# A fused two-layer network on one core: a transposed Q product, K and V in one product, earlier norm statistics, and a packed half tile

## What is computed

```python
x = x + attn(layernorm(x))     # 16 heads of 128, 4 K/V groups, causal softmax, projection
x = x + ternary(layernorm(x))  # a second layernorm, then a product with weights in {-1,0,1}
# linear attention, on layernorm(x):
QKV = einsum('bsd,ed->bse', X, W_in) + b_in
Q, K, V = split(QKV, 3)
Q, K = rope(Q, 128), rope(K, 128)          # only the first 128 of 256 features turn, in pairs
A = sum(K / norm(K) * V, axis=-2)          # one row of 256 numbers per batch
Y = einsum('bsd,ed->bse', A * Q, W_out) + b_out
x = x + Y + X
# gated layer, on layernorm(x), hidden size 704 = 5 tiles of 128 and one of 64:
x = x + qlinear(silu(qlinear(x, gate)) * qlinear(x, up), down)   # integer weights less 128, scaled
```

## Time and profile before

| | |
|---|---|
| median of three executions | 624.9 us |
| profiled execution, its span | 623.68 us, 621.9 us |
| TensorE busy | 582.7 us (94%), 4224 matmuls |
| VectorE busy | 507.0 us (82%), 1546 instructions |
| ScalarE busy | 361.3 us (58%), 1001 |
| GpSimd busy | 230.3 us (37%), 291 |
| share of the chain that ended last | TensorE 70%, VectorE 17%, ScalarE 5%, GpSimd 3% |

### The profile page before, as it was taken

The page is one execution under the profiler, slowest core; times in us unless marked ns, Lnnn a source line. Parts: engine busy times, 40 slices in busy tenths (PEclk is TensorE's granted clock), DMA queues, the critical chain, the costliest instruction groups (busy, mean ns, idle before and its releaser), DMA issues.

```text
span 621.9 us, 13094 instructions
## 1 busy us (share of the span) xinstructions
PE 582.7 (94%) x4224; PEld 545.5 (88%) x4224; DVE 507.0 (82%) x1546; ACT 361.3 (58%) x1001; POOL 230.3 (37%) x291
## 2 busy tenths in 40 slices
PE   8899999999999999999999999989758888799996
PEld 7799999999999999999999999989657777688785
DVE  4789789679878977987897798789969989878764
ACT  5776656656655765665676566568546243454452
POOL 4474223225222321422332142223657777402210
PEclk9999999999999999999999999999978999999998
DMA  8703100000000000000000000000000000001001
GB/s 326 250 1 140 69 2 2 1 1 0 0 0 0 0 0 0 0 0 0 0 0 0 0 0 0 0 2 0 2 1 0 1 1 1 3 1 35 34 14 54
DMA packets 7855, 14.63 MB, mean 24 GB/s; under 512 B 848, under 2 KB 5648, under 8 KB 7696
## 3 DMA queue, kind: packets, MB, share of 16 engines
q1 hardware_dynamic: 7824, 14.23, 6.3%
HBM read 12.13 MB, written 2.10 MB: 23 GB/s over the span
## 4 chain that ended last, share of the span: by engine, by line
PE 70%; DVE 17%; ACT 5%; issue 4%; POOL 3%; DVEq 1%; DMA 0%; ACTq 0%; POOLq 0%
PE bank L518 58%; PE bank L581 4%; PE bank L595 3%; ACT prob L931 3%; PE bank L528 2%; PE bank L598 2%; DVE pT L1165 2%; DVE xn L1159 2%; DVE prob L1384 2%; DVE prob L1231 1%; DVE prob L1210 1%; PE bank L687 1%; DVE stats L1148 1%; DVE ternary_stats L1328 1%; ACT qT L894 1%
## 5 line engine op out<-in xcount | busy, mean ns | idle before, releaser
L420 POOL TENSOR_SCALAR prob<-prob,rowinv 128x128 f32<-128x128 f32 (+1 forms) x128 | 106.5, 841 | 287.2 <-DVE rowinv L1228 287.2
L518 PE MATMUL bank<-xT,big 128*128 128x256 f32 x960 | 125.8, 283 | 0.6 <-DVE xT L1165 0.6
L931 ACT ACTIVATE prob<-prob,negmax 128x128 f32<-128x128 f32 (+1 forms) x256 | 112.9, 444 | 22.3 <-DVE negmax L1222 22.3
L518 PEld LDWEIGHTS bank<-xT,big 128*128 128x128 f32 x960 | 120.2, 192 | 1.5 <-issue 0.8
L518 PE MATMUL bank<-wp,oT 128*128 128x256 f32 x768 | 102.4, 283 | 0.0
L518 PEld LDWEIGHTS bank<-wp,oT 128*128 128x128 f32 x768 | 96.8, 191 | 0.6
L518 PE MATMUL bank<-pT,v 128*128 128x512 f32 (+1 forms) x384 | 81.3, 347 | 16.0 <-DVE pT L1165 13.0
L518 PEld LDWEIGHTS bank<-pT,v 128*128 128x128 f32 x384 | 63.9, 191 | 27.3 <-issue 7.5
L894 ACT ACTIVATE qT<-bank 128x512 fp32r<-128x512 f32 x68 | 40.6, 597 | 74.0 <-PE bank L518 72.5
L1165 DVE TENSOR_TENSOR pT<-bank,pT 128x512 fp32r<-128x512 f32 (+1 forms) x128 | 64.9, 548 | 1.9 <-ACT pT L894 1.9
L1165 DVE TENSOR_TENSOR qT<-bank,qT 128x512 fp32r<-128x512 f32 x68 | 46.8, 688 | 17.5 <-ACT qT L894 17.0
(11 more groups left out here) (132 smaller groups left out, 1038.5 us busy)
## 6 DMA issues: line engine op xcount, KB each, us to landing
x<-in_x SPq DMA_DIRECT2D x8, 256.0 KB, 8.2
raw<-in_wq SPq DMA_DIRECT2D x4, 512.0 KB, 8.2
raw<-in_wp SPq DMA_DIRECT2D x4, 512.0 KB, 8.0
out<-x SPq DMA_DIRECT2D x8, 256.0 KB, 2.1
raw<-in_w_gu SPq DMA_DIRECT2D x1, 1408.0 KB, 8.3
raw<-in_w_in SPq DMA_DIRECT2D x1, 768.0 KB, 4.6
raw<-in_w_down SPq DMA_DIRECT2D x1, 640.0 KB, 7.8
raw<-in_wk SPq DMA_DIRECT2D x1, 512.0 KB, 3.6
```

What stands on the lines that cost most here:

```text
L420: m = pool.tensor_scalar(prob[:, j % 2, 0, a:b], prob[:, j % 2, 0, a:b], rowinv[:, j % 2, r:r + 1], None, ALU.mult)
L518: m = pe.matmul(out, lhs(a), rhs(b), start=first and i == 0, stop=last and i == len(passes) - 1, skip_group_check=True)
L931: m = act.activation(prob[:, j % 2, i, a:b], prob[:, j % 2, i, a:b], ACT.Exp, scale=SCALE, bias=negmax[:, 2 * i + r:2 * i + r + 1], accum_ ...
```

## The change

- The input weights of Q and K are kept with the even features of each rope pair ahead of the odd ones (`by_pairs`, `by_halves`), and so are the rows of W_out. V is in the same order.
- Q is made transposed (features on the partitions) by `linear_q`: 12 matmuls of 256 columns into `bQ`, weights on the stationary side. So y is born transposed, and the transposes of y are gone. The rope of Q works on partitions: `q_products` on VectorE (one instruction of 128x256, two of 64x256), the sum on GpSimd (`q_rotate`). The bias of Q is added per partition.
- K and V are made by one product of 512 columns for each half, with one bias product of 512 columns; the banks alternate between (`bS0`, `bS1`) and (`bT0`, `bT1`) from batch to batch. ScalarE copies K out and squares it straight from PSUM; V stays in PSUM and kv reads it there. kv of batch `n` is made in the call of batch `n`.
- A, the sum of kv, is made as two columns with features on the partitions (`linear_sum`: 4 products of 1 column), copied by ScalarE, and used there as the scale with which Q is turned into the high part of y. The output of batch `n-1` is made in the call of batch `n`.
- The norm statistics of the linear stage are taken in attention: `linear_moments(n-1)` on VectorE and `linear_scale(n-1)` (seven small instructions) on GpSimd in step 7 of batch `n`. The scale and the mean of each batch are kept.
- The low parts of the gate and up weights are made on GpSimd in eight pieces of 352 columns instead of two of 1408; the low parts of the input weights move from VectorE to GpSimd.
- Gate and up of the last hidden tile (64 rows each) are one product of 128 rows. The high and the low part of its hidden values lie above each other in one tile of 128 rows, so one pass of the down product takes both.
- The linear stage is written out instead of a loop; constants for the transposed rope are made in batch 0.

The core of the diff (TensorE, then GpSimd, ScalarE, VectorE):

```diff
+                for k in range(KT):
+                    mm3(pe, out[:, :], lambda a: xTs[n % 2][:, a, k, t * P:(t + 1) * P], lambda a: lin_w[:, a, k, D:3 * D],
+                        k == 0, False)
+                pe.matmul(out[:, :], mean_rows, kv_bias, start=False, stop=True, skip_group_check=True).then_inc(s_kvp, 1)
...
-                for out, a0, a1 in ((bQK[t][:, :], 0, 2 * D), (v_bank(n, t), 2 * D, 3 * D)):
+                    pe.wait_ge(s_lqe, n)
+                    pe.wait_ge(s_lqc, n)
+                for e in range(2):
                     for k in range(KT):
-                        m = mm3(pe, out, lambda a: xTs[q][:, a, k, t * P:(t + 1) * P], lambda a: lin_w[:, a, k, a0:a1],
-                                k == 0, k == KT - 1 and a0 == 0)
-                for a in range(2):
-                    m = pe.matmul(v_bank(n, t), mean_rows, v_bias[:, a, :], start=False, stop=a == 1, skip_group_check=True)
-                m.then_inc(s_lp, 1)
+                        m = mm3(pe, bQ[:, e * S:(e + 1) * S], lambda a: lin_w[:, a, k, e * P:(e + 1) * P],
+                                lambda a: xTs[n % 2][:, a, k, :], k == 0, k == KT - 1)
+                m.then_inc(s_qTp, 1)
...
-                    pe.wait_ge(s_lY, n)
-                for t in range(ST):
-                    m = pe.matmul(bQ[:, 0:D], ones[:, :], kv[:, t, :], start=t == 0, stop=t == ST - 1)
+                if n == 0:
...
+                for e in range(2):
+                    for t in range(ST):
+                        m = pe.matmul(bO[:, e:e + 1], kv[:, t, e * P:(e + 1) * P], ones[:, 0:1], start=t == 0, stop=t == ST - 1)
                 m.then_inc(s_lA, 1)
...
+            def linear(n):
+                if n > 1:
+                    linear_kv(n, 0)
+                linear_transpose(n + 1) if n + 1 < NB else gated_transpose(0)
+                linear_sum(n - 1)
+                linear_kv(n, 1)
+                if n == 2:
+                    pe.wait_ge(s_lAc, n)
                     ternary_transpose(NB - 1)
...
+                if n == 3:
+                    pe.wait_ge(s_lAc, n)
+                    ternary(NB - 1, bO)
+                if n == NB - 2:
+                    pe.wait_ge(s_los, 4)
+                    pe.wait_ge(s_lAc, n)
+                    pe.matmul(bO[:, 8:12], ones[:, :], lo_sums[:, :], start=True, stop=True).then_inc(s_lop, 1)
...
+                if i == HT - 1:
+                    wait_apart(pe, s_gh, u - 1)
+                    for k in range(KT):
+                        mm = mm3(pe, bG[i % 2][:, :], lambda a: gate_up_last[a][:, k].rearrange("p g n -> p (g n)"),
+                                 lambda a: xT4[:, m, a, k, :], k == 0, k == KT - 1, PASSES[:1 + weight_parts])
+                    mm.then_inc(s_gg, 1)
+                    return
...
-                        mm = mm3(pe, bD[b][:, t * D:(t + 1) * D], lambda a: hT[i % 3][0:rows, a, at:at + P],
-                                 lambda a: down[0:rows, a, i, :], i == 0 and t == 0, i == HT - 1,
-                                 PASSES if weight_parts == 2 else PASSES[::2])
+                        if i == HT - 1:
+                            mm = mm3(pe, bD[b][:, t * D:(t + 1) * D], lambda a: hT[i % 3][:, 0, at:at + P],
+                                     lambda a: down[:, a, i, :], False, True, ((0, 0), (0, 1))[:weight_parts])
...
+            def gated_weights_lo(n, part):
+                src, (high, low), _ = LAYER_WEIGHTS[n]
+                at = slice(part * HID // 2, (part + 1) * HID // 2)
+                pool.wait_ge(s_lwhi, n + 1)
+                pool.tensor_tensor(low[:, at], src[:, at], f32(high[:, at]), ALU.subtract).then_inc(s_gwlo, 1)
...
+            def linear_scale(n):
...
+                    if last:
+                        if j in (2, 3):
+                            in_weights_lo(IN0 if j == 2 else IN1)
+                        if j == 5:
+                            linear_bias(0)
+                        if j >= 4:
+                            gated_weights_lo(GU0, j - 4)
+                    if j == J - 1 and not (isinstance(n, int) and n == 0):
+                        linear_scale(n - 1)
...
+            def linear(n):
+                if n == 1:
+                    inv_std_twice(NB - 1)
+                if n in (1, 2):
+                    gated_weights_lo(GU1, 2 * n - 2)
+                    gated_weights_lo(GU1, 2 * n - 1)
+                if n == 2:
                     ternary_bias(NB - 1)
+                if n == 4:
+                    linear_scale(NB - 1)
+                if n >= NB - 2:
+                    inv_std(n + 2)
+                k_rotate(n)
                 k_inverse(n)
...
+                q_rotate(n)
+                if n == 0:
+                    linear_bias(1)
+                if n < NB - 2:
                     linear_bias(n + 2)
...
+            def linear_y(n):
+                act.wait_ge(s_lA, n + 1)
+                if n > 0:
+                    act.wait_ge(s_lylo, n)
+                act.activation(A_sb[:, :], bO[:, 0:2], ACT.Copy).then_inc(s_lAc, 1)
+                act.wait_ge(s_lAc, n + 1)
+                act.wait_ge(s_lqr, n + 1)
+                if n > 0:
+                    act.wait_ge(s_lo, n)
+                for e in range(2):
+                    act.activation(yT[:, 0, e, :], q_sb[n % 2][:, e, :], ACT.Copy, scale=A_sb[:, e:e + 1]).then_inc(s_lyhi, 1)
+            def linear(n):
+                linear_k(n, 0)
+                linear_x_hi(n + 1, (n + 1) % 2) if n + 1 < NB else gated_x_hi(0)
+                linear_y(n - 1)
+                linear_k(n, 1)
+                if n == 2:
+                    ternary_hi(NB - 1)
+                linear_q(n)
+                if n == NB - 1:
                     gated_x_hi(1)
...
+            def linear_moments(n):
+                wait_apart(dve, s_fa, n + 1)
+                for t in range(ST):
+                    m = dve.bn_stats(l_stats[:, t, :], x_tile(n, t))
...
+                q = bQ[:, 0:S].rearrange("p (t s) -> p t s", t=ST)
+                dve.scalar_tensor_tensor(q_cos, q, q_bias[:, 0:1], cos_T, ALU.add, ALU.mult)
+                for e in range(2):
+                    into, of = slice(e * H, (e + 1) * H), slice((1 - e) * H, (2 - e) * H)
+                    m = dve.scalar_tensor_tensor(q_sin[into], q[of], q_bias[of, 0:1], sin_T[of], ALU.add, ALU.mult)
+                m.then_inc(s_lqc, 1)
...
-                    m = dve.scalar_tensor_tensor(kv[:, t, :], qkv[:, q, t, D:2 * D], k_inv[:, t:t + 1],
-                                                 qkv[:, q, t, 2 * D:3 * D], ALU.mult, ALU.mult)
+                    m = dve.scalar_tensor_tensor(kv[:, t, :], k_sb[n % 2][:, t, :], k_inv[:, t:t + 1],
+                                                 bKV[n % 2][t][:, D:2 * D], ALU.mult, ALU.mult)
...
+            def linear_y_lo(n):
+                for e in range(2):
+                    dve.wait_ge(s_lyhi, 2 * n + e + 1)
+                    m = dve.scalar_tensor_tensor(yT[:, 1, e, :], q_sb[n % 2][:, e, :], A_sb[:, e:e + 1],
+                                                 f32(yT[:, 0, e, :]), ALU.mult, ALU.subtract)
+                m.then_inc(s_lylo, 1)
+            def linear(n):
+                if n > 1:
+                    linear_x_lo(n + 1, (n + 1) % 2) if n + 1 < NB else gated_x_lo(0)
+                if n >= NB - 2:
+                    ln_moments(n + 2, n + 2 - NB)
+                linear_y_lo(n - 1)
+                k_cosine(n)
+                linear_apply(n + 2) if n < NB - 2 else gated_apply(n + 2 - NB)
+                q_products(n)
+                linear_kv(n)
+                if n == 1:
+                    linear_x_lo(2, 0)
+                    ternary_apply(NB - 1)
+                if n == 2:
+                    ternary_lo(NB - 1)
+                if n == 3:
+                    for i in (DOWN0, DOWN1):
+                        src, (high, low), _ = LAYER_WEIGHTS[i]
+                        dve.wait_ge(s_lwhi, i + 1)
+                        m = dve.scalar_tensor_tensor(low, src.bitcast(I32), -ZERO_POINT, f32(high), ALU.add, ALU.subtract)
+                    m.then_inc(s_dwlo, 1)
+                if n == NB - 1:
                     gated_x_lo(1)
...
+                add_bank(n - 1, bY, s_lo, s_lres, s_la)
+                if n == 3:
+                    add_bank(NB - 1, bO, s_fp, s_fb, s_fa)
+                    linear_moments(NB - 1)
```

673 lines of the change are left out of this document (355 added, 318 removed).

## The result

Four executions of the changed kernel took 613.26 to 616.55 us, median 614.95 us; four of the kernel before, beside them, 625.48 us. The ratio is 0.9843 (95% interval 0.9814 to 0.9872), so the change gives 10.5 us by the medians. The forecast was 605 us, a gain of 20: right in sign, inside the range, and nearly twice too large. The profiled execution is the slowest of the four, 616.55 us; its span is 614.7 us, and TensorE's mean granted clock is 0.979 (before 0.989).

The account below looks back on a forecast made before the run. Bounds: waits at attention's end, K's lane with TensorE close in the linear stage, TensorE in the gated stage. Savings 15.1 + 4.9 - 0.5 = 19.5 us cut span 621.9 to 602.4; plus 1.8 and 1.2: 605 us, range 598 to 614 (moved lock 597 to 616).

Parts of the forecast that it names:

- Batch 0: four more transposes and copies, 0.5 us more.: In batch 0 of attention, four added transposes and copies were to cost 0.5 us.
- From step 6 of attention to the gated layer: From attention's step 6 through the linear stage to the gated layer: 102.1 us before, 15 us less forecast.
- Last attention product at 452.4: End of attention: TensorE's last attention product was to start at 452.4 instead of 457.20.
- A new wait: Before linear call 2: TensorE waits 4.9 us for the low part of input 2, plus 2.0 for the lower clock.
- Calls 2 to 7, 52.9 and the 2.0: Linear calls 2 to 7: six of 7.6 us plus extras, 52.9 together; 2.0 for the lower clock after call 2's wait.
- Branch, two tiles, sum and output, 8.4: End of the linear stage: branch 2.0, two gate and up tiles 3.9, sum 0.6, output 1.5, wait 0.4; 8.4 us.
- Gated layer, 4.9 less.: Gated layer: three pairs each lose 1.45 us of matmuls, the last pair 0.5; 4.9 us less in all.
- An attention loop as long as before: Attention loop: statistics added in step 7 were to cost nothing; without cover 0.6 us a batch, 4 in all.
- The moved lock: Rival: GpSimd's work holds VectorE for 1.27 us in each linear call, 9 us in all, 614 us; chance 0.11.
- The clock as a slower rival: Rival: TensorE stays at 1.2 GHz after waits, each linear call costing 7.3 us more; three calls give 627 us; chance 0.03.

Follow-up runs that it names:

- e1: Changed kernel with batch 0's transposes of the constants and their copy placed behind step 3's output projection and output copy: 612.87 us, ratio 0.9789.
- e11: e8 plus VectorE's scale_eps of batch 0 placed ahead of step 3's row maxima: 600.47 us, ratio 0.9574.
- e3: Changed kernel with VectorE's low part of the down weights placed behind call 3's last ternary addition and linear statistics: 613.03 us, ratio 0.9792.
- e4: Changed kernel with GpSimd's additions to x waiting for the next pair's first xn in the middle gated pairs: 614.02 us, ratio 0.9805.
- e5: Changed kernel with the two statistics instructions of the linear norm issued twice for every batch: 615.7 us, ratio 0.9858.
- e7: Changed kernel with VectorE's low part of the K|V bias placed ahead of its normalisation in step 5 of the last batch: 616.39 us, ratio 0.9876.
- e10: Changed kernel with TensorE filled by identity transposes, 30 before call 2's first product and 20 before call 4's sums: 614.74 us, ratio 0.9827.
- e8: Changed kernel with e1, e3, e4, e7 and the early low part of call 2's input together: 600.22 us, ratio 0.9601.
- e9: e8 without the early low part of the K|V bias, so four of the five orders: 601.0 us, ratio 0.9604.

## Why the prediction was right in sign and off by half

The forecast's sum gave a span of 602.4 us, and the profiled one is 614.7. Of the 12.3 us between them 5.6 lie in batch 0, 3.5 between the end of attention and the gated layer, 1.8 in the gated layer, and 1.3 at the start, which scatters by as much.

- **"Batch 0: four more transposes and copies, 0.5 us more."** This step failed, and it alone holds nearly half of the error. Measured 6.1 us (46.90 to 53.03). It priced the added instructions by their length and did not ask what they wait for. TensorE's list has them ahead of step 3's attention product; they may write the bank only when VectorE has read the scale from it, and VectorE's `scale_eps` is its last work of step 3 (50.84). ScalarE's copy stands behind, 5.03 us, with the exps of the next step behind it. e1 and e11 take the cost away in two parts, 4.8 and 1.6.
- **"From step 6 of attention to the gated layer", 15 less.** Measured 11.6 (from first ternary statistics to tile 2: 462.54 before, 450.96 after). All times of after are taken 7.46 later below, the delay of its first statistics. *Last attention product at 452.4*: 453.8, since the half ahead of it waited for the bias and ran at the lower clock (2.85 us for what was put at 1.7). *"A new wait" of 4.9 and 2.0 for the clock*: right, 4.15 and about 1.5 (call 2 took 9.29: 7.4, 0.4 for the ternary transposes, the rest). *Calls 2 to 7, 52.9 and the 2.0*: 56.8 (477.16 to the end of call 7's products at 533.93). A call without anything in its way takes 7.40, kv 0.87: better than the 7.6 and 1.0 of the forecast. What was too small is call 4: 3.0 forecast, 6.9 measured. Its wait (3.63) was named with its cause. It is longer than it was priced, since the low part of the down weights took 2.91 us and not the 1.81 of the earlier trace rows; and the half clock behind it, about 3.3 us, which was charged at the first long wait, was forgotten at this one. e3 shows the size of both together, 5.7. *Branch, two tiles, sum and output, 8.4*: 9.0 (533.93 to 542.94).
- **"Gated layer, 4.9 less."** Measured 3.1. A pair was to take 17.4 and takes 18.42 (559.29 to 577.71, before 18.8). TensorE's products are 1.6 us shorter by their starts, but VectorE's xn, held beside GpSimd's additions, is awaited 1.17 instead of 0.58, and the other 0.6 us of the loss goes in smaller gaps, half of it ahead of the next pair's first product (572.51). The hold itself is not new: xn took 2.02 us before. The earlier trace rows priced the products; TensorE "busy for 18.22 of 18.8" was read as the bound, without asking how far VectorE was behind it. With that hold gone (e4) a pair takes 17.5, the forecast's figure.
- **"An attention loop as long as before"**: right, 54.09 us a batch in both kernels. e5 shows that the cover is nearly used up: a second pair of statistics costs 0.19 us a batch.
- *Rivals.* The moved lock was put in the linear calls. There kv and the low part of y are free (0.87 and 0.89). In call 3 the cosines and the normalising are held beside GpSimd's rope (0.69 and 1.36 us, at 492.06 and 492.67, against 0.42 and 0.74), but TensorE does not wait for them. The hold that costs time is the one on xn in the gated loop. It stood there before the change (2.02 us), and the packing only uncovered it. The Trainium skill, page "SBUF — State Buffer", section "Who interferes with whom", says that a `tensor_scalar` in a two-port mode and a `tensor_tensor` with two SBUF inputs can be blocked by GpSimd; the trace agrees with both, xn 1.99 beside GpSimd's additions against 0.73 without them (e4), and the low part of hidden 1.73 beside them (e4) against 0.68. The clock as a slower rival did not decide the sign, but it took part of several gains: in e1, e3, e7 and e10 the profiled execution lost at one place what it had won at another.

## What to carry to other kernels

An added instruction is priced by its wait before its length: read what it needs, where that stands in the other engine's list, and what stands behind it. A stretch in which one engine is busy for 97% can still hold a second engine that is half a microsecond behind, and a cut of a microsecond uncovers it. On a kernel whose clock falls at waits, judge an order by the marks in the trace as well as by the time, and split a stretch before calling it unchanged: in e5 the clock's luck covered a real cost. Remove several waits together, too: alone each gave 2.4 to 3.8 us or nothing, five together 15.1.

## What the runs showed of the hardware

- The same wait does not always have the same clock behind it. Ahead of the first K|V half TensorE stood 2.75 us in the changed kernel and 2.74 in e5; behind it the half took 2.85 and 1.63 us. Ahead of call 2's sums TensorE stood 1.56 us in e8, 1.57 in e9 and 1.54 in e11. Behind it the half of the product took 2.91 us in e8, 1.63 in e9 and 1.93 in e11.
- Behind a wait of 4.15 to 4.19 us the lower level (1.2 GHz) ended within call 2's first half in the changed kernel and lasted through its second half in e3 and e7, 3 us of difference.
- The branch on TensorE costs 2.2 to 3.8 us in which the trace mostly shows nothing that is waited for. From its end to tile 2 it took 6.6 us at full clock, and up to 9.2 where part of it ran at the lower one. The code of this place is the same in all runs of the changed kernel.
- While VectorE and GpSimd both work on SBUF, either can be the one that is held. Before, GpSimd's 128x2 instruction at 478.92 took 1.50 us beside VectorE's low part of the down weights (1.81), where it takes 0.22 elsewhere; after, VectorE's low part took 2.91 beside GpSimd's addition (1.27).
